# Row maxima to the score stack: by DMA in place of TensorE transposes and a copy

## The reference

```python
qkv = x @ attn_qkvw + attn_qkvb            # x is layer-normed
scores = einsum('bhqd,bhkd->bhqk', q, k) * scale
probs = softmax(scores, axis=-1)
ctx = einsum('bhqk,bhkd->bhqd', probs, v)
```

## Time and profile before

| | us |
|---|---|
| median of 3 runs | 3738.44 |
| profiled execution, device time | 3735.51 |
| its span | 3733.8 |
| TensorE busy | 3329.8 (89%) |
| VectorE busy | 2358.1 (63%) |
| ScalarE busy | 1747.4 (47%) |
| GpSimd busy | 1807.8 (48%) |
| mean granted TensorE clock | 0.957 |

### The profile page before, as it was taken

How to read it: one execution, slowest core, us unless ns; L and a number is a source line. 1 busy time by engine, 2 the same in 40 slices (tenths; PEclk the granted TensorE clock), 3 DMA queues, 4 the chain that set the end, 5 groups by cost and what they waited for, 6 DMA issues and landing times. The chain is left out here.

```text
span 3733.8 us, 66940 instructions
## 1 busy us (share of the span) xinstructions
PE 3329.8 (89%) x25160; PEld 1743.2 (47%) x25160; DVE 2358.1 (63%) x4410; ACT 1747.4 (47%) x2240; POOL 1807.8 (48%) x1913
## 2 busy tenths in 40 slices
PE   0899999999999999999984999988878888757999
PEld 0344555555545555555542555544444454433444
DVE  8377777777777777777776677755666656552222
ACT  3267777777767777776673221213333333330000
POOL 2366676666766767666662122214433333321333
PEclk9999999999999999999996999999988999977999
DMA  4111111111111111111114454431222222113443
GB/s 169 28 39 51 46 43 51 46 46 47 44 50 50 41 50 44 51 41 38 39 42 141 154 170 162 164 114 51 74 85 75 91 91 74 73 46 145 152 152 118
DMA packets 198464, 297.85 MB, mean 80 GB/s; under 512 B 33297, under 2 KB 147985, under 8 KB 197138
## 3 DMA queue, kind: packets, MB, share of 16 engines
q1 hardware_dynamic: 193490, 276.96, 22.7%
q10 hardware_dynamic: 4608, 16.78, 1.1%
q0 software_dynamic: 64, 0.01, 0.0%
HBM read 142.62 MB, written 100.67 MB: 65 GB/s over the span
## 5 line engine op out<-in xcount | busy, mean ns | idle before, releaser
L685 DVE TENSOR_REDUCE nmax<-ring_ps 128x1 f32<-128x512 f32 x1024 | 686.3, 687 | 313.1 <-PE ring_ps L509 287.2
L773 POOL TENSOR_TENSOR elo<-e,ehi 128x1024 f16<-128x1024 f32 x256 | 607.8, 2374 | 529.5 <-ACT ehi L635 529.5
L568 PE MATMUL proj_ps<-xnT,wqk 128*128 128x512 f16 x3072 | 748.7, 380 | 3.3 <-DVE xnT L736 2.5
L629 ACT ACTIVATE e<-st_ps,exp_scale 128x1024 f32<-128x1024 f32 x512 | 570.5, 1114 | 349.5 <-PE st_ps L529 292.6
L635 ACT ACTIVATE ehi<-st_ps,exp_scale 128x1024 f16<-128x1024 f32 x512 | 569.8, 1113 | 125.2 <-PE ctx_ps L549 122.9
L568 PEld LDWEIGHTS proj_ps<-xnT,wqk 128*128 128x128 f16 x3072 | 299.0, 97 | 373.4 <-issue 6.4
L1454 PE MATMUL f_ps<-wT,fxT 128*128 128x512 f16 x1536 | 370.8, 399 | 35.8 <-DVE fm L1628 19.7
L546 PE MATMUL ctx_ps<-v_sb,ehi 128*128 128x65 f16 x4096 | 374.5, 193 | 25.1 <-DVE sums L718 14.9
L529 PE MATMUL st_ps<-qs,ks 98*128 98x512 f16 x1024 | 391.3, 382 | 2.3 <-ACT ehi L635 2.2
L509 PE MATMUL ring_ps<-ks,qs 96*128 96x512 f16 x1024 | 388.8, 380 | 1.6 <-DVE nmax L685 1.3
L546 PEld LDWEIGHTS ctx_ps<-v_sb,ehi 128*128 128x128 f16 x4096 | 298.4, 97 | 182.2 <-DVE sums L718 72.8
(11 more groups left out here) (218 smaller groups left out, 4532.7 us busy)
## 6 DMA issues: line engine op xcount, KB each, us to landing
x<-x_scratch SPq DMA_DIRECT2D x64, 512.0 KB, 4.4
qs<-qk_hl SPq DMA_DIRECT2D x768, 32.0 KB, 1.9
ks<-qk_hl SPq DMA_DIRECT2D x768, 32.0 KB, 1.9
ctx_scratch<-ctx SPq DMA_DIRECT2D x64, 256.0 KB, 2.5
ct<-ctx_scratch SPq DMA_DIRECT2D x32, 512.0 KB, 4.7
xb<-in_L_attn_a_x_dram SPq DMA_DIRECT2D x32, 512.0 KB, 4.5
x_scratch<-xb SPq DMA_DIRECT2D x32, 512.0 KB, 2.6
xT_scratch<-xT SPq DMA_DIRECT2D x32, 512.0 KB, 3.1
```

Of the source, the lines that this page charges most:

```text
L568: mm = pe.matmul(proj_ps[:], wqk[:, wp, c, H * qk + P * g:H * qk + P * g + P], xnT[:, b % 2, xp, c, :], start=(n == 0), stop=(n == 23))
L629: nc.scalar.activation(e32[:, half], st_ps[:, half], ACT.Exp, scale=exp_scale[:, 0:1]).then_inc(e32_done, 1)
L685: dve.tensor_reduce(nmax[:, h % 2, c:c + 1], ring_ps[:, ring_max(h, c) % 2, :], AX.X, ALU.max, negate=True).then_inc(ring_free, 1)
L773: nc.gpsimd.tensor_tensor(elo[:, h % 2, 2:4, :], e32[:, 1], ehi[:, h % 2, 2:4, :], ALU.subtract).then_inc(elo_pool, 1)
```

## The change

The maxima reach the stack by two DMAs a head. So that these write contiguous runs, tokens are laid out four to a partition: x is loaded with token 4q+t on partition q of tile t (`x_s`), `xnT` is written with a step of four tokens so that its free axis is still in natural order, and the queries of `max_scores(h, c)` are those with number 4q+c, read from qs with a step of four elements (`qs_v`). Partition q of `nrow` then holds the maxima of queries 4q to 4q+3: eight bytes for the high and eight for the low part, and a DMA moves 128 such pieces into one partition of qs.

The transposes (`max_rows`), the copy (`row_stack`) and the f16 identity go; a head takes four turns of `ring_ps`. `scores(h, 0)` waits for the DMAs (`row_in`). In SP's queue `rows(s + 2)` stands at the end of each slot, behind `stacks` and `context` in slot i = 3. Since a tile of x now holds tokens from the whole sequence, V units must wait for all four tiles of their batch; the two transposes of the last tile of a batch move to steps 14 and 15 of one group.

```diff
+    x_s = x.rearrange("b (p t) h -> b t p h", p=P)
...
-                nrow = sb(p1, "nrow", [P, 2, T, 2], F16)
-                ident16 = sb(p1, "ident16", [P, P], F16)
+                nrow = sb(p1, "nrow", [P, 2, 2, T], F16)
...
+                xnT_v = xnT[:].rearrange("p b l c (q t) -> p b l c t q", t=T)
+                qs_v = qs[:].rearrange("p r (q t) -> p r t q", t=T)
...
+                row_in = [sem(f"row_in{i}") for i in range(2)]
...
                 def ring_max(h, c):
-                    return c if h == 0 else 5 * h - 1 + (c if c < 2 else c + 1)
-
-                def ring_row(h):
-                    return 5 * h + 6 if h < TOT - 1 else 5 * TOT - 1
+                    return T * h + c
...
+                turned_in = {}
+                for n in range(FIRST, B * T):
+                    for half in range(2):
+                        m, at_sub = (turn_group(n) + half, 15) if n % T < T - 1 else (turn_group(n), 14 + half)
+                        turned_in.setdefault(m, []).append((at_sub, n, half))
...
                         def load_x(n):
...
-                            sp.dma_start(xt[:, n % 2], x_t[n // T, n % T]).then_inc(xt_in, 16)
+                            sp.dma_start(xt[:, n % 2], x_s[n // T, n % T]).then_inc(xt_in, 16)
...
+                        def rows(h):
+                            if not live(h):
+                                return
+                            sp.wait_ge(row_done, h + 1)
+                            wait(sp, st_full, 2 * (h - RING + 1))
+                            for part in range(2):
+                                sp.dma_start(qs[3 * HD + part:3 * HD + part + 1, h % RING, :], nrow[:, h % 2, part, :]).then_inc(row_in[h % 2], 16)
...
                         for s in SLOTS:
                             m, i = s // GH, s % GH
                             if s < 0:
+                                rows(s + 2)
                                 continue
...
                                 stacks(m + 2)
                             if i == 3 and m >= 1:
                                 context(m - 1)
+                            rows(s + 2)
...
-                            pe.matmul(ring_ps[:, ring_max(h, c) % 2, :], qs[0:3 * HD, h % RING, P * c:P * c + P],
+                            pe.matmul(ring_ps[:, ring_max(h, c) % 2, :], qs_v[0:3 * HD, h % RING, c, :],
                                       ks[0:3 * HD, h % RING, :], start=True, stop=True).then_inc(ring_full, 1)
-
-                        def max_rows(h):
...
                             if c == 0:
-                                pe.wait_ge(ring_free, ring_row(h) + 1)
+                                pe.wait_ge(row_in[h % 2], 32 * (h // 2 + 1))
...
+                                if a == 0 and half == 0:
+                                    if b < 2:
+                                        pe.wait_ge(x0_lo, 2 * min(T * (b + 1), FIRST))
+                                    if b > 0:
+                                        pe.wait_ge(split_done, place["T", T * b + T - 1, 1] + 1)
...
-                                if c == 1:
-                                    max_rows(s + 1)
                                 weighted(s - 2, c)
...
                             dve.wait_ge(ring_free, ring_max(h, T - 1) + 1)
-                            dve.tensor_scalar(nrow[:, h % 2, :, 0], nmax[:, h % 2, :], 1.0 / ONES_ROW, None,
+                            wait(dve, row_in[h % 2], 32 * (h // 2))
+                            dve.tensor_scalar(nrow[:, h % 2, 0, :], nmax[:, h % 2, :], 1.0 / ONES_ROW, None,
                                               ALU.mult).then_inc(row_hi, 1)
...
-                        def row_stack(h):
...
-                                if c == 1:
-                                    row_stack(s + 1)
...
-                                hi, lo = (xnT[:, b % 2, part, 4 * half:4 * half + 4, P * t:P * t + P] for part in range(2))
+                                hi, lo = (xnT_v[:, b % 2, part, 4 * half:4 * half + 4, t, :] for part in range(2))
```

More of the change, by code:

```diff
@@ L406, in turn_group @@
                     return G * (b - 1) - 3 + 2 * t
-                turned_in = {turn_group(n) + half: (n, half) for n in range(FIRST, B * T) for half in range(2)}
+                turned_in = {}
[3 more added lines that the diff above has]
+                        turned_in.setdefault(m, []).append((at_sub, n, half))
                 def units_of(m):
@@ L432, in hybrid_layer @@
                         splits[at(16 * m + 5 * j + 5)] = u
-                    if m in turned_in:
-                        u = ("T",) + turned_in[m]
+                    for at_sub, n, half in turned_in.get(m, []):
+                        u = ("T", n, half)
                         order.append(u)
-                        turns[at(16 * m + 15)] = u
-                        splits[at(16 * m + 18)] = u
+                        turns[at(16 * m + at_sub)] = u
+                        splits[at(16 * m + at_sub + 3)] = u
                 place = {u: i for i, u in enumerate(order)}
@@ L454, in xT_first @@
                 def xT_first(t, part, half):
-                    return xnT[:, t // T, part, 4 * half:4 * half + 4, P * (t % T):P * (t % T) + P]
+                    return xnT_v[:, t // T, part, 4 * half:4 * half + 4, t % T, :]
                 def bank_first(t, half):
@@ L508, in max_scores @@
                             wait(pe, ring_free, ring_max(h, c) - 1)
-                            pe.matmul(ring_ps[:, ring_max(h, c) % 2, :], qs[0:3 * HD, h % RING, P * c:P * c + P],
+                            pe.matmul(ring_ps[:, ring_max(h, c) % 2, :], qs_v[0:3 * HD, h % RING, c, :],
                                       ks[0:3 * HD, h % RING, :], start=True, stop=True).then_inc(ring_full, 1)
-                        def max_rows(h):
-                            if not live(h):
-                                return
-                            pe.wait_ge(row_done, h + 1)
-                            wait(pe, ring_free, ring_row(h) - 1)
-                            rows = ring_ps[:, ring_row(h) % 2, :].bitcast(F16)
-                            for c in range(T):
-                                mm = pe.transpose(rows[0:2, P * c:P * c + P], nrow[:, h % 2, c, :], ident16[:])
-                            mm.then_inc(ring_full, 1)
                         def scores(h, c):
@@ L571, in unit @@
                                 b, t, half = u[1:]
-                                if a == 0 and half == 0 and T * b + t < FIRST:
-                                    pe.wait_ge(x0_lo, 2 * (T * b + t + 1))
-                                elif a == 0 and half == 0:
-                                    pe.wait_ge(split_done, place["T", T * b + t, 1] + 1)
+                                if a == 0 and half == 0:
[3 more added lines that the diff above has]
+                                        pe.wait_ge(split_done, place["T", T * b + T - 1, 1] + 1)
                                 for n in range(a, z):
@@ L607, in _ @@
                                 turn_first(T + i)
-                        pe.wait_ge(const_done, 4)
+                        pe.wait_ge(const_done, 3)
                         pe.wait_ge(x0_lo, 2 * FIRST)
@@ L691, in row_parts @@
                             dve.wait_ge(ring_free, ring_max(h, T - 1) + 1)
[L692 removed]
+                            wait(dve, row_in[h % 2], 32 * (h // 2))
+                            dve.tensor_scalar(nrow[:, h % 2, 0, :], nmax[:, h % 2, :], 1.0 / ONES_ROW, None,
                                               ALU.mult).then_inc(row_hi, 1)
                             dve.wait_ge(row_hi, h + 1)
[L695 to L703 removed]
+                            dve.scalar_tensor_tensor(out=nrow[:, h % 2, 1, :], in0=nmax[:, h % 2, :], scalar=1.0 / ONES_ROW,
+                                                     in1=nrow[:, h % 2, 0, :], op0=ALU.mult, op1=ALU.subtract).then_inc(row_done, 1)
                         def lo_exps(h):
@@ L823, in split @@
                                     if b == 0:
-                                        pool.wait_ge(const_done, 4)
+                                        pool.wait_ge(const_done, 3)
                                     else:
```

10 lines of the change are left out of this document (1 added, 9 removed).

## The result

The changed kernel takes 4175.27 us (median of 4 runs, 4171.99 to 4177.10) against 3737.69 us (3736.43 to 3740.38, 4 runs): ratio 1.1169, 95% interval 1.1149 to 1.1188. That is 438 us slower; the forecast was 384 us slower, 4120 us with a range of 3995 to 4235. The profiled execution took 4171.99 us, its span is 4170.3 us, and its mean granted clock is 0.907.

The account below looks back on a forecast made before the run. TensorE was taken to bound phase 1. 62 blocks x (4.5 us longer loop + 1.7 us clock loss) = 384 us, added to 3735.5, gave about 4120 us; own range 4060 to 4185, with two rivals 3995 to 4235.

Parts of the forecast that it names:

- SP's queue sets the loop: SP's queue: row DMAs behind 24 stack DMAs come late, so the loop goes from 28.86 to 33.4 us, +4.5 a group.
- The chain: From row_done through SP's row, stack and context issues to landing: scores(4m+5, 0) can run at t0 + 20.55 us.
- t0: Start of step 12 of a 16-step group (four heads, four steps each); from one to the next took 28.86 us.
- Only head 4m+5: TensorE stands still some 6.6 us before this head's first scores, once a group; rows of 4m+6 and 4m+7 are in time.
- Landing: Row DMA of 128 pieces of 8 bytes, from issue to landing: 2.3 us, bounds 1.9 and 4.
- rival 3: Row DMAs run piece by piece on one engine, 6.1 us each; every slot about 15 us, about 5700 us; 5%.
- The clock: TensorE's clock falls to the lower level after each stall: 1.7 us a group, ends 0 and twice that.
- The rest of the loop: TensorE from step 4, where the stall ends, to the next t0: 12.85 us without clock loss.
- Row_done of head 4m+4: Last VectorE piece of this head's rows, which SP waits for before its row DMAs: t0 - 0.14 us.
- The layout: Strided writes of xnT, on GpSimd and in the prologue on ScalarE and VectorE: 0 to 3 us in all.
- The strided weight loads: Weights of max_scores read with a step of 8 bytes on TensorE: 0 to 0.5 us a group, taken as 0.
- Rival 1: Rows of head 4m+5 land by t0 + 13.9, no stall; 1.76 us a group gained, about 3627 us; 6%.

## Why the prediction was right, point by point

The mechanism was the one forecast, at its place, in all its steps, and the time is within the range, 55 us above the forecast.

- *SP's queue sets the loop.* Shown from three sides: the queue changed (-489 us), the block shortened by eight issues (the gap falls by 5.0 us), the order turned (the stall moves to the next head). The chain came out with an error of 0.2 us in 20.6, in part by luck: the row DMA was issued 0.4 us later than forecast (t0 + 18.65 for 18.25) and landed 0.3 faster. The 15.8 us that the prediction gives as the mean of the blocks before are 16.0 in the trace; after, they are 15.9.
- *Only head 4m+5.* Right; moving its two DMAs alone takes away all but some 20 us of what moving all does.
- *Landing.* 2.3 was forecast from the earlier trace rows, 2.0 measured. The stack DMAs take 1.9: 128 pieces of 8 bytes land like pieces of 1 KB. With the Trainium skill's rule on the number of engines (DMA: Bandwidth & Descriptors, "Why a DMA increments its semaphore by 16 and not by 1") the trace agrees as far as it shows it: the 16 increments of a row DMA come one by one, the first 1.56 us after the issue and the last 0.34 us behind it, in the median. But the price of rival 3 was wrong whatever the number: a packet of 8 bytes takes 9 ns in the trace, and not the 48 taken as a bound from the bias load, so 128 in a row on one engine would be 1.1 us (an estimate) and not 6.1. The Trainium skill's sentence that the time to start a DMA is usually small relative to the DMA (same page, "Issuing engines are not separate DMA queues") doesn't hold for this block: an issue is 0.63 us, a third of a landing of 2.0, and there are 24 in a row.
- *The clock: mis-sized.* 1.7 us a group was taken from the earlier trace rows; it is 2.2, by the stretch from the scores to the next t0 with the stall filled (12.86 us) and empty (15.04). Over 62 groups that is some 30 us of the 55 that the forecast lacked.
- *The rest of the loop.* Without the clock's loss the stretch to t0 is 12.86 us, as forecast (12.85). Row_done of head 4m+4 comes at t0 + 0.18 and not at t0 - 0.14. The earlier trace rows show only the second of the two row instructions, which is still 0.16 us long there; the first takes 0.80 us in the mean for these heads and took 0.32 before, when row_done came at t0 - 0.29. I had taken it as unchanged.
- *The layout: the step that failed.* "The strided writes of xnT fall on GpSimd (30% idle), on ScalarE and VectorE only in the prologue: 0 to 3 us in all" is wrong. With the rest of the layout they cost 47 us alone, 21.5 of them GpSimd's by the run with plain writes. In the changed kernel most of it lies under the stall, so that it did the sum little harm. GpSimd's idle share was no cover, since the price isn't paid by GpSimd's queue but by VectorE, on the path of TensorE (last section). The part in the prologue alone was 5 us in the run of the layout. The strided weight loads cost at most 0.01 us a step (a step with a projection takes 1.962 us against 1.953), within the 0 to 0.5 us a group that the prediction allowed.
- *Rival 1 (rows in time) was priced too low*: 3627 us, where runs without the stall take 3682 to 3686. Removed work of 1.76 us a group was worth 0.82.

## What to carry to other kernels

A DMA that something waits for soon must not stand behind a block of DMAs that nothing waits for: count the issues ahead of it in its queue, at the price of an issue, before counting its landing. Two DMAs of 33 in a group, moved to another engine's queue turned +12% into -1%. A stall of TensorE as long as this one costs its own length and then the clock; and an access pattern that slows an engine with time to spare can still slow the engine that has to wait for its instructions.

## What the runs showed of the hardware

**Some VectorE instructions and GpSimd's casts and subtractions exclude each other.** The first row instruction reads and writes four numbers a partition. In 300 to 1800 us of the kernel after it takes 0.17 us in the 53 cases in which GpSimd isn't casting or subtracting; beside GpSimd's subtraction into v_sb (37 cases) it takes 0.31 in the mean, into qk_hl (42) 0.80, into xnT (22) 1.10, beside the cast into xnT (14) 1.30. In each slow case it ends 0.02 to 0.03 us after GpSimd's instruction does. One case, VectorE and then GpSimd:

```profile
1017.90 1.16 DVE L696 TENSOR_SCALAR nrow<-nmax 128x4 f16<-128x4 f32 x1
1019.10 0.16 DVE L699 SCALAR_TENSOR_TENSOR nrow<-nmax,nrow 128x4 f16<-128x4 f32 x1
```

```profile
1017.68 1.35 POOL L824 TENSOR_TENSOR xnT<-stage,xnT 128x512 f16<-128x512 f32 x1
```

GpSimd ends at 1019.03, VectorE at 1019.06. The mean of the instruction is 0.216 us before, 0.574 after, 0.698 with the rows on ScalarE's queue, 0.549 with GpSimd's plain writes, and 0.212 where it stands behind the copy of the sums. The rows above stand by themselves; the Trainium skill (SBUF — State Buffer, "SBUF: two separate sides") describes a shared pair of ports that GpSimd's instruction or one of certain VectorE instructions, whichever starts first, holds for its whole length; the trace agrees, with the case above as its number. So a longer GpSimd instruction is paid for in VectorE's queue. VectorE's row maxima (TENSOR_REDUCE) aren't held up: 0.688 us in the mean of all 1024, 0.687 before.

It works both ways, and who starts first decides. Both engines subtract their half of the exponentials at the start of a slot. In the kernel before, at one such place, VectorE starts first, takes 1.22 us, and GpSimd 3.02:

```profile
534.80 1.22 DVE L709 TENSOR_TENSOR elo<-e,ehi 128x1024 f16<-128x1024 f32 x1
534.98 3.02 POOL L773 TENSOR_TENSOR elo<-e,ehi 128x1024 f16<-128x1024 f32 x1 [1.53 <-ACT ehi L635]
```

With the layout alone GpSimd starts first at the same place of the program, takes 2.12 us, and VectorE 2.87, for which TensorE then waits (the 1.9 us above). Over the whole of that run VectorE takes 1.28 us in the mean in the 239 overlapping cases in which it starts first, and 2.87 in the 7 in which GpSimd does, whose own then takes 2.12 for 2.43:

```profile
547.93 2.12 POOL L781 TENSOR_TENSOR elo<-e,ehi 128x1024 f16<-128x1024 f32 x1 [1.33 <-ACT ehi L643]
548.27 2.87 DVE L717 TENSOR_TENSOR elo<-e,ehi 128x1024 f16<-128x1024 f32 x1
```

**Writes with a step of 8 bytes aren't free.** GpSimd's cast of 128x512 to f16 took 1.33 us with the step and 0.61 without; VectorE's copy of 2x512 from PSUM 1.30 and 0.42. With the same step in TensorE's weight loads a step of the loop was at most 0.01 us longer.

**The clock's loss depends on the gap.** With stalls of 6.4 us in the mean once a group the granted clock fell in all 43 groups between 250 and 1800 us, at 2.2 us each in what follows; with stalls of 1.4 us in the mean it fell five times in the same stretch, and with the stall filled or gone not once.
